# Cross-attention and routed FFN: VectorE's own first guess for the LayerNorm roots, and another order of the routing rounds

## The reference

```python
x = x + xattn(ctx, ctx, layernorm(x))     # x (16, 256, 128), ctx (16, 64, 128), one head, D = 128
x = x + ffn(layernorm(x))
# xattn: kp = k Wk', vp = v Wv' + bv, qp = q Wq' + bq
#        softmax(qp kp' / sqrt(D)) vp Wo' + bo
# ffn:   p = softmax(xt Wr + br); top 2 of E = 8 experts, their probabilities made to sum to 1
#        h_e = LN(relu(xt W1_e + b1_e)) * g1_e + be1_e      # D -> F = 512
#        y_e = LN(relu(h_e W2_e + b2_e)) * g2_e + be2_e     # F -> D
#        out = sum over the two experts of probability * y_e
```

## Time and profile before

| | |
|---|---|
| median of 3 runs | 329.19 us (328.3, 329.69, 329.19) |
| profiled execution, first to last instruction | 268.4 us |
| median less span | 60.8 us |
| busy TensorE, VectorE, ScalarE, GpSimd | 239.9, 229.7, 211.5, 190.6 us |
| mean granted clock of TensorE | 0.955 of full speed |

### The profile page before, as it was taken

The page is one execution under the profiler, slowest core; times in us unless marked ns, Lnnn a source line. Parts: engine busy times, 40 slices in busy tenths (PEclk is TensorE's granted clock), DMA queues, the critical chain, the costliest instruction groups (busy, mean ns, idle before and its releaser), DMA issues.

```text
span 268.4 us, 10286 instructions
## 1 busy us (share of the span) xinstructions
PE 239.9 (89%) x2960; PEld 194.0 (72%) x2960; DVE 229.7 (86%) x1091; ACT 211.5 (79%) x795; POOL 190.6 (71%) x300
## 2 busy tenths in 40 slices
PE   1989779899888677679899999999999999999994
PEld 1564567777666434579899979999999999999330
DVE  0667986867689989689999988999999999999875
ACT  2465675789888888757999988999999999999700
POOL 8602277877757777775888888888888888878640
PEclk9997995899999759999999999999999999999999
DMA  6998398123425234354333443333315686772257
GB/s 159 313 299 295 91 271 279 51 89 92 139 82 136 83 91 99 84 119 94 84 90 67 89 82 81 73 72 75 84 33 142 155 155 141 149 143 86 68 187 233
DMA packets 48676, 34.56 MB, mean 129 GB/s; under 512 B 26871, under 2 KB 42743, under 8 KB 48620
## 3 DMA queue, kind: packets, MB, share of 16 engines
q1 hardware_dynamic: 38972, 22.80, 32.8%
q0 software_dynamic: 6592, 9.00, 12.7%
q10 hardware_dynamic: 3056, 2.11, 2.6%
HBM read 15.11 MB, written 12.02 MB: 101 GB/s over the span
## 4 chain that ended last, share of the span: by engine, by line
DVE 37%; issue 22%; PE 20%; ACT 9%; DMA 5%; DVEq 4%; SPq 1%; ACTq 0%
PE bank L721 15%; DVE vo L1873 8%; PE bank L725 4%; DMA w2f<-in_L_ffn_W 3%; DVE rs L1914 3%; DVE cx L1903 3%; DVE kq L1866 3%; DVE w2f L1653 3%; DVEq L1880 2%; DVE st L1891 2%; ACT ex L1175 2%; DVE mv L1897 1%; DMA wr<-in_L_ffn_Wr 1%; ACT xt L1198 1%; DVE topi L1573 1%
## 5 line engine op out<-in xcount | busy, mean ns | idle before, releaser
L679 POOL DMA_INDIRECT answers<-vo,words_of x71 | 70.6, 994 | 23.8 <-issue 19.4
L667 POOL DMA_INDIRECT slot_rows<-pay,pos x64 | 65.5, 1023 | 27.9 <-issue 18.5
L721 PE MATMUL bank<-kb_room,w1h 128*128 128x128 f16 x568 | 55.2, 219 | 1.7 <-issue 1.7
L725 PE MATMUL bank<-w2h,rh 128*128 x284 | 51.4, 219 | 1.6 <-ACT w2l L1122 1.6
L725 PE MATMUL bank<-rh 128*128 128x129 f16 x284 | 51.5, 220 | 0.0
L725 PE MATMUL bank<-w2l,rh 128*128 x284 | 51.4, 219 | 0.0
L721 PE MATMUL bank<-kb_room,w1l 128*128 128x128 f16 x284 | 51.2, 219 | 0.0
L1866 DVE SCALAR_TENSOR_TENSOR kq<-bank,rh 128x512 f16<-128x512 f32 x71 | 47.8, 673 | 0.1
L721 PEld LDWEIGHTS bank<-kb_room,w1h 128*128 x568 | 43.6, 98 | 2.6 <-issue 2.6
L1347 ACT ACTIVATE rh<-bank 128x512 f16<-128x512 f32 x71 | 41.1, 579 | 5.2 <-PE bank L721 4.2
L705 POOL DMA_DIRECT2D words_of<-slot_rows x71 | 40.8, 576 | 2.0 <-issue 1.8
(11 more groups left out here) (259 smaller groups left out, 601.7 us busy)
## 6 DMA issues: line engine op xcount, KB each, us to landing
x_tok<-in_x SPq DMA_DIRECT2D x8, 256.0 KB, 7.7
w1f<-in_L_ffn_W SPq DMA_DIRECT2D x2, 1024.0 KB, 8.8
pay<-pay SPq DMA_DIRECT2D x8, 256.0 KB, 3.3
w1f<-answers SPq DMA_DIRECT2D x8, 256.0 KB
w2f<-answers SPq DMA_DIRECT2D x8, 256.0 KB, 2.9
kb_room<-slot_rows SPq DMA_TRANSPOSE x71, 3.3
words_of<-slot_rows POOLq DMA_DIRECT2D x71, 1.0 KB
answers<-vo,words_of POOLq DMA_INDIRECT x71
```

Source lines behind the costliest of these rows:

```text
L667: eng.indirect_dma_start(slot_words, bass.IndirectOffsetOnAxis(ap=pos[:, g % 2, k, i:i + 1], axis=0), pay[g % 2][:, k, i, :].bitcast(U32), ...
L679: eng.indirect_dma_start(answers, bass.IndirectOffsetOnAxis(ap=words_of[:, j % NW, 0:1], axis=0), z[j % NZ], None).then_inc(s_ans[j % NZ], 16)
L721: return eng.matmul(dst, lhsT, rhs, start=start, stop=stop)
L725: return eng.matmul(dst, lhsT, rhs, start=start, stop=False, skip_group_check=True)
```

## The change

VectorE makes the root's first guess itself, from the bits of the variance (`guess`), in place of ScalarE's exponential; the first of the two Newton steps has other constants. The number of Newton instructions stays. In rounds above 2 (groups 4 to 8 counted from 1), `normed(n)` goes behind the roots, and the maxima of group n+1 are taken in round n, behind `top_mask`; `pay_lo` and `gate_rows` go behind `picked` and `pos_`. On ScalarE `x2_copy` goes ahead of `pay_hi`, and some weight pieces go between `xT_copy` and `pT_copy` (`AMID`). TensorE's, GpSimd's and SyncE's programs stay, but for a memset. The diff, cut to its core:

```diff
+    ROOT_BITS = float(0x5F1FFFF9)
+    ROOT_STEPS = ((-0.703952253, 0.703952253 * 2.38924456), (-0.5, 1.5000003))
...
-        DOWN_SQUARES = {2: (0, 1), 3: (2, 3)}
-        UP_SQUARES = {3: (0,), 4: (1, 2, 3)}
-        UP_HI = {5: (0, 1, 2), 6: (3, 4, 5, 6)}
-        DOWN_HI = {7: (1, 2, 3)}
+        AMID, AFTER = 0, 1
+        DOWN_SQUARES = {(2, AFTER): (0, 1), (3, AMID): (2,), (3, AFTER): (3,)}
+        UP_SQUARES = {(3, AFTER): (0,), (4, AMID): (1,), (4, AFTER): (2, 3)}
+        UP_HI = {(5, AFTER): (0, 1), (6, AMID): (2,), (6, AFTER): (3, 4), (7, AMID): (5, 6)}
+        DOWN_HI = {(7, AFTER): (1, 2, 3)}
...
 scalar:
-            root1_guess(0)
...
-            root1_guess(1)
...
             for n in range(1, GROUPS + 1):
-                if n <= 2:
-                    root2_guess(n - 1)
                 if n < GROUPS:
                     probs(n)
-                if n > 2:
-                    root2_guess(n - 1)
-                if n == 7:
-                    w_up(7)
-                    w_down(0)
...
                 if n < GROUPS - 1:
                     xT_copy(n + 1)
+                weights(n, AMID)
+                if n == 7:
+                    w_up(7)
+                    w_down(0)
                 if 2 < n < GROUPS:
                     pT_copy(n)
                 xt_(n - 1)
                 if n == 2:
                     pT_copy(2)
+                if 2 < n < GROUPS:
+                    x2_copy(n)
                 pay_hi(n - 1)
                 gate_exp(n - 1)
                 if n == 1:
                     pT_copy(1)
-                if n < GROUPS:
+                if n <= 2:
                     x2_copy(n)
...
+                weights(n, AFTER)
 vector:
+            def guess(y_, v):
+                return eng.tensor_scalar(y_.bitcast(I32), v.bitcast(I32), -0.5, ROOT_BITS, ALU.mult, ALU.add)
...
-            def stats2(g, scores=None):
-                if scores is not None:
-                    maxima(scores)
+            def stats2(g):
                 eng.wait_ge(s_x2, g + 1)
                 for i in range(GT):
                     t = eng.bn_stats(st[:, i, :], x2[:, g * GT + i, 0:D])
-                    if i == 0 and scores is not None:
-                        max_scaled(scores)
...
-                if g >= 1:
-                    eng.wait_ge(s_guess2, g)
-                eng.tensor_scalar(ve2[:, :], mv[:, :, 1], EPS, None, ALU.add).then_inc(s_var, 1)
+                stat.up(eng.tensor_scalar(ve2[:, :], mv[:, :, 1], EPS, None, ALU.add))
+                eng.wait_ge(q_stat, stat.n)
+                root2.up(guess(y2[:, :], ve2[:, :]))
...
             for n in range(1, GROUPS + 1):
-                stats2(n - 1, n if 2 < n < GROUPS else None)
+                stats2(n - 1)
                 weights(n, 2)
-                if 2 < n < GROUPS:
-                    normed(n)
                 if n <= 2:
                     max_(n)
                 for k in range(7):
...
+                if 2 < n < GROUPS:
+                    normed(n)
                 logits(n - 1)
...
                 if n == GROUPS - 1:
                     words(0)
+                if 2 < n + 1 < GROUPS:
+                    max_(n + 1)
+                weights(n, 16)
+                picked(n - 1)
+                weights(n, 17)
+                pos_(n - 1)
+                weights(n, 18)
                 pay_lo(n - 1)
-                weights(n, 16)
+                weights(n, 19)
                 gate_rows(n - 1, 0)
-                weights(n, 17)
-                picked(n - 1)
+                weights(n, 20)
                 gate_rows(n - 1, 1)
-                weights(n, 18)
-                pos_(n - 1)
-                weights(n, 19)
+                weights(n, 21)
                 gate_rows(n - 1, 2)
-                weights(n, 20)
-                weights(n, 21)
```

More of the change, by code:

```diff
@@ L365, in build @@
                      "key_bias1", "keys1", "sdT1", "values1", "values2")
-        p_setup, c_setup, c_exp, c_wrc, c_wkq, s_var1, s_guess1, s_sd, s_sel = (signal(n) for n in (
-            "pe_setup", "act_setup", "exp_loaded", "wr_centred", "wkq_centred", "var1_eps", "rstd1_guess", "sd1",
+        p_setup, c_setup, c_exp, c_wrc, c_wkq, s_sd, s_sel = (signal(n) for n in (
+            "pe_setup", "act_setup", "exp_loaded", "wr_centred", "wkq_centred", "sd1",
             "bias_rows"))
@@ L382, in build @@
         q_wkq = signal("chain_wkq")
-        p_xT, s_xT, p_score, s_smax, s_prob, s_norm, p_pT, s_pT, p_attn, s_var, s_x2, s_guess2, s_xt, s_hi, s_lo, \
+        p_xT, s_xT, p_score, s_smax, s_prob, s_norm, p_pT, s_pT, p_attn, s_x2, s_xt, s_hi, s_lo, \
             s_mask, p_rank, s_pos, p_base = (signal(n) for n in (
-                "pe_xT", "xT", "pe_score", "nmax", "exp", "normed", "pe_pT", "pT", "pe_attn", "var2", "x2",
-                "rstd2_guess", "xt", "pay_hi", "pay_lo", "mask", "pe_rank", "pos", "pe_base"))
+                "pe_xT", "xT", "pe_score", "nmax", "exp", "normed", "pe_pT", "pT", "pe_attn", "x2",
+                "xt", "pay_hi", "pay_lo", "mask", "pe_rank", "pos", "pe_base"))
         s_copy = [signal(f"pay_copy{n}") for n in range(2)]
@@ L598, in gpsimd @@
             eng.memset(onesb[:, :], 1.0)
-            eng.memset(guess0[:, :], 0.5 * LN2 * (BIAS - 0.043)).then_inc(s_ones, 1)
-            for n in range(2):
-                eng.memset(second[:, n:n + 1], float(n))
+            eng.memset(second[:, 0:1], 0.0).then_inc(s_ones, 1)
+            eng.memset(second[:, 1:2], 1.0)
             eng.memset(be2_diag[:, :], 0.0).then_inc(s_diag, 1)
@@ L1277, in scalar, with weights @@
             x2_copy(0)
-            root1_guess(1)
             key_bias(1)
+            def weights(n, place):
+                for c in DOWN_SQUARES.get((n, place), ()):
+                    square_sum(1, w2_flat, w1h, c)
+                for c in UP_SQUARES.get((n, place), ()):
+                    if c == 0:
+                        eng.wait_ge(ld_b1, 16)
+                        eng.wait_ge(s_w1x, E)
+                    square_sum(0, w1f[:, :], w1l, c)
+                for e_ in UP_HI.get((n, place), ()):
+                    w_up(e_)
+                for e_ in DOWN_HI.get((n, place), ()):
+                    w_down(e_)
             for n in range(1, GROUPS + 1):
-                if n <= 2:
-                    root2_guess(n - 1)
                 if n < GROUPS:
                     probs(n)
-                if n > 2:
-                    root2_guess(n - 1)
-                if n == 7:
-                    w_up(7)
-                    w_down(0)
                 if n == 8:
@@ L1319, in scalar @@
                     eng.wait_ge(ld_w2[1], 16)
[L1320 to L1327, removed]
+                if n == 5:
                     eng.wait_ge(s_scale, 1)
@@ L1468, in var1_ @@
                 eng.wait_ge(q_stat, stat.n)
-                eng.scalar_tensor_tensor(out=ve1[:, tiles], in0=within[:, tiles], scalar=1.0 / D, in1=apart2[:, tiles],
-                                         op0=ALU.mult, op1=ALU.add).then_inc(s_var1, 1)
+                stat.up(eng.scalar_tensor_tensor(out=ve1[:, tiles], in0=within[:, tiles], scalar=1.0 / D,
+                                                 in1=apart2[:, tiles], op0=ALU.mult, op1=ALU.add))
             def root1_(n):
@@ L1486, in max_ @@
             def max_(g):
-                maxima(g)
-                max_scaled(g)
-            def maxima(g):
                 eng.wait_ge(p_score, g + 1)
```

35 lines of the change are left out of this document (10 added, 25 removed).

## The result

**338.2 us** (335.63 to 340.88), against 328.75 (328.09 to 329.69) for the kernel before in runs beside it: ratio 1.0242, 95% interval 1.0155 to 1.0328, slower by more than 0.5%. I had forecast 331.1, with 333.2 as the upper end.

A forecast was written before the change was run, and what follows sets the result against it. The FFN runs at VectorE's unchanged pace, so its start, set by a ring of four engines, decides. Delays through the rounds bring the hand-over 1.9 us late: span 268.4 to 270.3, plus 60.8 gives 331.1 us; 8-in-10 range 327.2 to 333.2.

The forecast's parts named there:

- the scores end 2.94 later, at 54.0: Round 3: TensorE ends group 4's scores 2.94 us after `probT(3)` at 51.05; VectorE idles 0.9 for them.
- my walk: Round-by-round following of the engines' waits before the FFN, against the kernel before; ends with the hand-over 1.9 us late.
- a rival in round 7: TensorE stands about 4 us before `probT(7)`; half clock doubles the last weight pieces and `up(0)`: 332.9 us; chance 0.10.
- Round 2: VectorE idles 2.7 us for group 3's scores, against 0.51 before; round 3 starts at 45.3, 2.0 late.
- my second rival: TensorE's clock falls a little later than group 3's scores; first stand 1 us shorter, 330.1 us; chance 0.22.
- The ring of rounds 3 to 8: Engines waiting on each other before the FFN: rounds 4 to 8 start 1.6, 1.7, 0.7, 1.4 and 2.0 us late.
- The wait of `squared` in round 5: VectorE waits 1.5 us inside round 5's roots, because `weight_scale(0)` needs TensorE's `totals`, reached at 69.4.
- GpSimd's group 4: GpSimd's payload of group 4, released by the gates, comes 1.8 us later, near 79, as late as the FFN.
- The guess: VectorE's own first guess of the root costs 0.2 us a round, bounds 0.1 and 0.3, and removes ScalarE's trip.
- The handing on: Between round 8 and the first FFN matmul nothing takes up the delay; the hand-over comes 1.9 us late.
- The 60.8 us around the span: Time outside the traced span of 268.4 us, taken as unchanged and added to the predicted span of 270.3.
- The first rival (faster): VectorE finds the scores finished each time, so early maxima cost only 0.2 a round: -2.8 us, 326.4; chance 0.20.

The follow-up runs named there:

- the squares later: Kernel before, with ScalarE's first two squares of W2 moved behind the exponentials of group 3: 269.6 us, ratio 0.996; second kind of chip 329.8 us, 1.001.

## Why the prediction was wrong

- **The step that failed: round 3, "the scores end 2.94 later, at 54.0".** The 2.94 came from a stretch at full clock, where `probT(3)` followed the idle matmuls without a pause, and I moved it behind a pause and kept its length. Measured on the first kind of chip: 5.1 us, scores at 56.5, `smax` waits 3.19 and not 0.9, and `ranks` and the weight pieces behind it are slow too (from `probT(3)` to `probT(4)` 13.9 us; 10.4 in my walk). The trace of the result, from the second kind, has the same 5.1 us. Filling the pause gave the step back at its forecast size. The pause itself was mis-sized as well: my walk leaves TensorE some 1.5 us (to 51.05, from 49.6 where the idle matmuls of before end), since it took the stretch at half clock ahead of them for a fixed part of the round; that stretch came earlier and the pause was 5.58. I had the mechanism, as a rival in round 7 with a chance of 0.10, on the argument that "nothing in the rows says that a longer one prolongs it". But the question was not whether the fall lasts longer; it was whether a new pause makes a new one, and where the critical chain then is. In round 7, where I priced it, the pause (4.50) came and cost little.
- **What is not shown: that this pause made the fall near 50 us.** The same fall came at 50.2, 50.3 and 49.8 in the traces of the guess alone, of both orders undone and of the squares later, behind 1.27, 1.69 and 0.52 us before `probT(3)`; in all three the clock had been at half around 33 to 40 before, as in the changed kernel. There `probT(3)` came at 47.5, 48.0 and 46.5, ahead of the fall; the new order puts it behind. What is shown is that the scores ran at half clock there, that idle matmuls in the pause kept the clock up, and that the earlier probabilities bring the time down.
- The rule of the Trainium skill, "TensorE: Matmul & The Clock Gate", section "HAM oscillation", says that pauses bring the throttle back and the work behind them runs cold; it spoke against this order, and the windows of this case agree: 0.51 at and behind a pause of 5.58 us, 1.00 when it was filled. How long a pause must be no run here shows, and it is not the length alone: falls came behind 1.66 us (before, 39.4) too.
- **Round 2, right in kind, its size in part by luck.** Forecast: 2.7 us idle before `smax`, round 3 at 45.3. Measured: 2.13, 45.5. Round 2 began 1.0 us earlier than before and not 0.63, and 0.70 went at once into a wait for group 2's scores (35.15) that I did not have. The scores of group 3 ran at full clock, which my second rival asked for, and still ended at 41.9, the time of the walk. The whole wait of 9.1 us at `rsum` went, down to one of 0.9.
- **The ring of rounds 3 to 8, right within 0.7 us a round given the clock** (round 5 lasted 12.4 in the kernel with more idle matmuls, forecast 11.75). The wait of `squared` in round 5 was forecast at 1.5 and was 1.23 in the changed kernel, 1.35 in the filled one. GpSimd's group 4 came at 84.67 (77.70 before), as late as the FFN, as argued.
- **The guess**, 0.2 a round, was mis-sized: 0.33 in rounds 3 to 6. That adds 0.5 to the sum.
- **The handing on.** From round 8 to the first FFN matmul 11.0 us, before and after; nothing took up the delay, as forecast.
- **The 60.8 us around the span** were no constant: where trace and time are of one execution, 1.6 us lie around the span. They are the difference of two kinds of chips.
- **The first rival (faster)** had VectorE find the scores ready. With the probabilities ahead again it does so in round 3 (53.50), though not in rounds 2 and 4, and the kernel is still not faster.
- **Still open: the 9.5 us of the second kind of chip.** The first FFN matmul came at 146.9 in the changed kernel, and at 145.7 in the kernel with the squares later, which takes the time of before there. From there to the end the one took 191.2 and the other 182.4. So by these two executions most of that chip's loss lies in an FFN whose instructions are the same, at the standstills without a releaser. The failed step stands in that chip's trace too (5.1 us), but how much of the 9.5 it makes is not shown. The runs that would have tested one order alone there fell on chips of the first kind. No run tells why the standstills grew.

## What to carry to other kernels

A wait that is taken from one engine lands on another. Where it lands on TensorE, price the matmuls behind the new pause at half the clock as well, and look first whether the chain to the next round runs through them. The test is cheap: the same order, with idle matmuls in the pause. It gave back 4 of the 6 us; putting the producer (here one reciprocal and one product) ahead of the pause gave back as much without them. And where a fixed load holds a round, look at it before the clock: with the load's squares in their old place an earlier round 2 and a fuller clock gave nothing, and moving them brought round 4 forward by 1.5 us, though the time as a whole is not shown to be less.

## What the runs showed of the hardware

- The same kernel before took 268.7 to 276.9 us in 29 runs beside the last four kernels. With the mean granted clock at 0.932 in one and at 0.961 in another of the first runs it took 273.0 and 269.2: where TensorE's clock falls differs from execution to execution and moves the time by more than 1%. One profile of such a kernel is one draw; the round starts of two kernels compare cleanly only when their falls stand at the same places (as they did up to round 8 for before and the changed kernel with the probabilities ahead: 39.4 and 90.6 in both). Both traces of the changed kernel have other falls (from 32.2, 49.2, 76.6 and 97.0, within 1.2 us of each other), so its starts in the table carry these as well.
- Two kinds of chips, 272 and 329 us for one program. On the slower one ScalarE and VectorE stand where nothing in the trace releases them, TensorE at times takes one instruction in 0.7 us, and added instructions of TensorE cost more: 74 more idle matmuls took the kernel with the squares later from 329.8 to 336.7 there, and from 269.6 to 272.0, ratios 0.996 and 0.998 with overlapping intervals, on the other.
- One and the same instruction, the guess on a tile of 128 x 4, took 0.17 us in rounds 1, 2 and 8 of the changed kernel and 0.30 to 0.31 in rounds 3 to 6; no run tells why.
